# A gated cross-attention block with a quantized feed-forward: the feed-forward's groups of batches cut as 3, 3, 2 instead of 2, 3, 3, and its steps placed anew

## The reference

```python
x = x + tanh(g_xattn[0]) * xattn(ctx, ctx, layernorm(x), Wk, Wv, bv, Wq, bq, Wo, bo)
x = x + tanh(g_ffn[0])   * ffn(layernorm(x), w1, conv_w, conv_b, w2)

# xattn: single head of width 512
scores = (q @ Wq.T + bq) @ (k @ Wk.T).T / sqrt(512)
out    = (softmax(scores) @ (v @ Wv.T + bv)) @ Wo.T + bo

# ffn: 512 -> 2048 -> 512
act_quant(x):    scale = 127 / max|row|, round, clip to -128..127, / scale
weight_quant(w): scale = 1 / mean|w|, round, clip to -1..1, / scale
h = act_quant(x) @ weight_quant(w1).T
h = silu(depthwise conv of width 3 along the 100 rows, + conv_b)
y = act_quant(h) @ weight_quant(w2).T
```

## Time and profile before

| | us |
|---|---|
| median of 3 runs | 359.85 |
| the three runs | 353.22, 360.3, 359.85 |
| the profiled execution, its own time | 355.76 |
| its span | 353.9 |

### The profile page before, as it was taken

One profiled execution on the slowest core, in us unless ns is written; L12 is line 12 of the kernel. 1 busy time (PEld: TensorE's weight loads), 2 busy tenths in 40 slices (PEclk: granted clock), 3 DMA queues, 4 the chain that ended last, 5 costly groups with the idle time before them and its releaser, 6 DMA issues.

```text
span 353.9 us, 4349 instructions
## 1 busy us (share of the span) xinstructions
PE 293.7 (83%) x1565; PEld 206.8 (58%) x1565; DVE 184.7 (52%) x390; ACT 154.0 (44%) x255; POOL 99.5 (28%) x96
## 2 busy tenths in 40 slices
PE   4957999989988989758988996776978897868695
PEld 2427899656536766537767784544836854434342
DVE  0094232330225127577577347489857545897562
ACT  3003228684367552588541234198731102976000
POOL 1008000024210980234214003053420802544070
PEclk9995599999999999985999998799988589999899
DMA  6998139806696259500240600000000000000002
GB/s 194 235 247 342 53 110 272 192 1 154 159 417 152 60 119 252 142 0 3 74 95 5 164 2 0 0 3 23 2 23 0 0 0 25 1 24 25 0 0 69
DMA packets 27950, 32.19 MB, mean 91 GB/s; under 512 B 17865, under 2 KB 17865, under 8 KB 26778
## 3 DMA queue, kind: packets, MB, share of 16 engines
q1 hardware_dynamic: 27930, 31.93, 33.0%
HBM read 26.09 MB, written 1.64 MB: 78 GB/s over the span
## 4 chain that ended last, share of the span: by engine, by line
PE 22%; DVE 15%; issue 12%; ACT 6%; POOL 3%; DVEq 0%; POOLq 0%; ACTq 0%
PE pvb L592 4%; PE yb L667 3%; DVE a L1093 3%; DVE u L1086 3%; PE ff L641 2%; DVE acc_q L1098 2%; ACT z L823 2%; PE yb L462 2%; ACT ab L817 2%; PE tr L552 2%; PE yb L464 1%; PE yb L463 1%; PE tr L676 1%; PE yb L627 1%; PE sc L571 1%
## 5 line engine op out<-in xcount | busy, mean ns | idle before, releaser
L873 POOL TENSOR_TENSOR z<-a,ab 128x300 f32<-128x300 f32 (+1 forms) x48 | 34.4, 716 | 67.7 <-DVE a L1093 67.7
L592 PE MATMUL pvb<-pt,ctx 120*128 120x100 f32 (+1 forms) x384 | 50.1, 293 | 1.8 <-ACT pt L754 1.8
L592 PEld LDWEIGHTS pvb<-pt,ctx 120*128 120x128 f32 (+1 forms) x384 | 49.0, 209 | 3.5 <-issue 3.4
L641 PE MATMUL ff<-xqt,w1t 128*128 128x300 bf16 (+1 forms) x192 | 30.4, 291 | 16.6 <-DVE u L1086 14.3
L571 PE MATMUL sc<-kt,qm 128*100 128x361 f32 x128 | 42.5, 481 | 0.0
L815 ACT ACTIVATE a<-u,convb,conv 128x300 f32<-128x300 f32 (+1 forms) x48 | 28.9, 602 | 15.5 <-DVE u L1086 15.2
L641 PEld LDWEIGHTS ff<-xqt,w1t 128*128 128x128 bf16 x192 | 17.2, 103 | 27.3 <-DVE u L1086 21.6
L552 PE MATMUL tr<-ident,ctx 120*128 120x120 f32 (+1 forms) x192 | 29.4, 276 | 4.1 <-ACT kt L733 3.2
L990 DVE COPY kt<-tr 128x361 f32<-128x361 f32 x32 | 17.0, 533 | 27.9 <-PE tr L552 24.8
L1093 DVE SCALAR_TENSOR_TENSOR a<-u,conv,a 128x297 f32<-128x297 f32 (+1 forms) x48 | 30.4, 633 | 1.2 <-ACT a L815 0.9
L571 PEld LDWEIGHTS sc<-kt,qm 128*100 128x100 f32 x128 | 21.1, 170 | 16.6 <-issue 2.5
(11 more groups left out here) (158 smaller groups left out, 480.4 us busy)
## 6 DMA issues: line engine op xcount, KB each, us to landing
ctx<-in_ctx_dram SPq DMA_DIRECT2D x16, 720.0 KB
wraw<-in_L_ffn_w_dram SPq DMA_DIRECT2D x8, 1024.0 KB, 12.6
x_sb<-in_x_dram SPq DMA_DIRECT2D x2, 800.0 KB
out_dram<-x_sb SPq DMA_DIRECT2D x8, 200.0 KB
wq_sb<-in_L_xattn_Wq_dram SPq DMA_DIRECT2D x4, 256.0 KB, 4.4
wk_sb<-in_L_xattn_Wk_dram SPq DMA_DIRECT2D x4, 256.0 KB, 5.4
wv_sb<-in_L_xattn_Wv_dram SPq DMA_DIRECT2D x1, 1024.0 KB, 5.0
wo_sb<-in_L_xattn_Wo_dram SPq DMA_DIRECT2D x1, 1024.0 KB, 8.4
```

The lines of the kernel that those rows point to most:

```text
L592: mm = nc.tensor.matmul(pvb[:, k * S:(k + 1) * S], cx[b % NCTX][0:r, i, k * P:(k + 1) * P], pt[0:r, i, :], start=(i == 0), stop=(i == 5))
L641: mm = nc.tensor.matmul(ffb[j % 2][:, 0:w], w1t[:, j * DK + k, :], xqt[:, k, 0:w], start=(k == 0), stop=(k == DK - 1))
L873: nc.gpsimd.tensor_tensor(z[:, q, 0:w, i].rearrange("p (b s) -> p b s", b=nb), a1[:, n % NBUF, 0:w].rearrange("p (b s) -> p b s", b=nb), a ...
```

## The change

```diff
-GROUPS = [(0, 2), (2, 5), (5, 8)]
+GROUPS = [(0, 3), (3, 6), (6, 8)]
...
-FILL_CUTS = [17, 22, 33, 50, 60, 77, 89, 92]
+FILL_CUTS = [17, 22, 23, 35, 51, 57, 77, 92]
```

## The result

The changed kernel takes 381.43 us (median of 4 runs, 380.39 to 382.81), the kernel before 358.32 (4 runs; with the fourth its median fell from the 359.85 shown above). The ratio is 1.0725, 95% interval 1.0626 to 1.0824: slower. Executions of one kernel fall into a faster and a slower state; the ratios and intervals here are of the faster ones alone, the medians of all, so that 381.43 over 358.32 is 1.0645. The forecast was 373.4 us, slower, range 362 to 384. Direction and place were right, the time was short by 8 us: from the same median a rise of 15.1 us was forecast and 23.1 measured.

What follows compares the result with a forecast made beforehand. TensorE bounds pure attention, VectorE feed-forward, chains of short steps the end. Span 353.9 + 9.5 (wait) + 3 (clock) + 5.1 (groups) = 371.5 us, with 1.9 more 373.4 us; range 362 to 384.

Steps and rivals of the forecast that it cites:

- Part 1: SP's queue: the moved weight step holds batch 4's context load, so that batch's first key step starts +9.5 us later.
- Part 2: TensorE's clock after 11.5 us of idle waiting for batch 4's context: half speed, +3 us (0 to 8).
- `pv.7`: Ahead of group 1's feed-forward: two of the four `pv.7`, `xqt` and its copy, and half clock, 5.5 us.
- Part 3: Segments behind the start of batch 4's keys: 216.8 us against 211.7, +5.1 us (-5 to +10).
- `ff.1`: Group 1's feed-forward tiles, 300 wide with three `f2` and three `out`: 32.7 us.
- `ff.2`: Group 2's feed-forward tiles, 200 wide: 24.5 us (22 to 26.7).
- `ff.0`: Group 0's feed-forward tiles, 300 wide, beside `pt`, `pv` and `scores`: 30.5 us (28 to 32.2).
- stage 5: From batch 6's first key step to batch 7's, with `am2` and four `quant`: as the 19.1 us before.
- the chain to `ff.2`: End of `y.7` to group 2's first feed-forward tile, `quant` exposed: 22.6 us (11.4 if all hid, 25 if nothing interleaves).
- A: Rival at SP's queue, 131 to 143 us: context load isn't held, not slower, 360.9 us; chance 0.13.
- B: Rival: group 1's quantization hides beside `y.7`, the 22.6 us shrink to 13, 363.8 us in all; chance 0.12.
- C: Rival: TensorE's half clock lasts, 5 us more behind `kt.4` and 3 in `pv.7` and the `f2`, 381 us; chance 0.15.

Runs made afterwards that it cites:

- the base: The changed kernel, its list of steps untouched, with SP issuing batch 4's context load ahead of the last transposing DMA: 366.73 us, ratio 1.0233.

## Why the prediction was right in kind and wrong in size

- **Part 1, the wait: right.** Place, order and length. Forecast 11.5 us of wait and +9.5 from `kt.3` to `kt.4`; measured 12.5 and +10.4, at the upper bound of 10.4. The missing 0.9 us is that between the end of the traffic and the semaphore: the step "keeps the DMA engines busy until 181.1, which is 8.3 us" took traffic for landing. The bound of 9.07 from before's `kt.4` was the better value. The prediction also read one row of the Trainium skill ("DMA: Bandwidth & Descriptors", Bandwidth) by its rate alone. Its two figures do not agree with each other: 1 MB in 6.15 us is 163 GB/s (170 if a MB is 2^20 bytes) and not 341. By that time 1.44 MB would take 8.4 to 8.9 us, an estimate from the page, and the 8.3 us of this trace agree with it; only the rate differs.
- **Part 2, the clock behind the wait: right.** 3 forecast, 2.6 measured (20.07 against 17.48 in the base). The advice of the Trainium skill ("TensorE: Matmul & The Clock Gate", What's actually happening), 3.5 at most, agrees with this one wait. For the kernel as a whole it does not: in the kernel before, `pv.7` alone took 9.85 us in place of 5.57, 4.3 more.
- **Part 3, the groups: the step that failed.** "+5.1" came out at +11.3 (from `kt.4` to the end 225.6, less 211.7 of before, less the 2.6 of the clock); the base, which has no wait, shows +11.6 (223.3 less 211.7). That its median is only 8.1 over the kernel before fits: it gains 2.4 from `kt.3` to `kt.4` (16.56 against 18.92), starts `kt.3` 1.9 later, and the profile of before lies 2.6 under its median. Terms: `ff.1` +4.1, `ff.2` +2.2, `ff.0` +2.0, stage 5 +1.3, the chain to `ff.2` +1.0; smaller than forecast were `pv.7` (-1.8), the stretch ahead of it (-1.0) and that to `f2 all` (-2.1).
 - `ff.1`: I priced the third `f2` at 1.5, by adding to `ff.2` of before, which took 31.2 with two, hardly more than the 30.55 that `ff.1` takes here with none. `f2` in `ff.1` cost 2.1 each on average: 30.55 without, 36.85 with three, and 36.21 with three at full clock. Why two cost so little there stays open.
 - `ff.2`: in the changed kernel its second `f2`, at 349.1, took 5.06 us in place of 3.62, mostly at half clock; at a granted clock of 1.00 `ff.2` took 25.0 (in the run with `f2` moved), near the 24.5 forecast.
 - `ff.0`: I took the `f2` and `out` of before's `ff.1` off its 32.2. It came out at 32.5 without them, so they had cost little there. That they hid behind attention's steps is my reading; no run tests it.
 - Stage 5: its granted clock was 0.92, against 1.00 in the 19.1 of before. What of the 1.3 us this is, and where the 1.0 in the chain to `ff.2` lies, no run shows.
- **The start.** 2.9 us of the profiled execution's loss lie ahead of the first changed step. In the profiles of the twelve experiments, whose steps are the same up to there, `kt.3` starts between 123.9 and 125.6; the profile of before, 123.25, was an early one. Up to 26.9 us its granted clock was 1.00, in the changed kernel's profile 0.95. So the profile to which I added was 2.6 us under the median of its kernel, and I had said up to 4. This part of the shortfall is the spread between executions and not the change.
- **Rivals.** A (no wait) fell at the timeline; its time of 360.9 for the grouping alone was 6 us too low against the base's 366.7. B (`quant` hides) fell: 23.6 us to `ff.2`, as forecast. C (half clock lasts) was half right, and that its 381 us is the time measured is luck. It added 5 us behind `kt.4` on top of the 3, and 2.6 was all that came; the missing microseconds were in the groups and the start. Behind the wait the clock was back within 6 us, but `ff.1` to `ff.2` holds further stretches at half clock, with a granted clock of 0.69 and 0.71 over 29 us.

By single changes: the moved step alone loses 11.1 us in the kernel before, the grouping without the wait 8 us by the medians (1.0233), together 19; the change lost 23.1 by the medians, and 22 to 29 by the interval of its ratio. Together they lose more in part because in the changed order `ln2` no longer stands in front of `kt.4`: without the wait, `kt.3` to `kt.4` takes 16.56 us there and 18.92 in the old order, with it 29.3 and 29.4, so the wait costs 12.7 us in the changed order and 10.5 in the old one.

What is open: why two `f2` at the same tiles meet a full clock in one kernel and a half clock in the other, and why the load in the run with the step put back was waited for until 11.0 us after its issue. It was not alone: batch 5's load was issued 3.4 us behind it. But so it was in the kernel before, where TensorE read the context after 9.07 us.

## What to carry to other kernels

When a step is moved, follow what its last consumer queues behind it: here a 2 us step held a cast, the cast a transposing DMA, and this, only by the order of one issuing queue, a load that TensorE needed next. Issue loads with a near deadline ahead of DMAs with a far one. A stretch with two pieces in it gives no price for a third: measure the stretch with none as well. And count a landing to the semaphore, not to the end of the traffic.

## What the runs showed of the hardware that I had not expected

- The same 48 `pv.7` matmuls, back to back, took 5.5 to 5.6 us in two kernels and 9.8 to 10.45 in four others, at 2.4 and 1.2 GHz. Once at half clock, they stayed there to their end, though TensorE did not rest (10.45 us busy out of 10.45, clock 0.50). Ahead of them TensorE had waited: 2.05, 0.84 and 0.91 us in the kernel before, 6.26 and 2.16 in the run with `quant` beside `pv.7`. Short filler matmuls of 512 columns in these waits kept the full clock. The Trainium skill ("TensorE: Matmul & The Clock Gate", What's actually happening) has sustained work release the clock; here that was not so for these 100-column float32 matmuls, and full again it was only in `y.7` or behind it.
- A context load of 1.44 MB showed 8.4 us of traffic and 0.9 us more until a waiting queue went on; from issue to TensorE's start it took 9.4 us in two kernels and 11.0 in a third.
